# The last 64 gate rows and the last 64 up rows of an FFN share one chunk of TensorE's columns

## What is computed

```
DIM = 256;  HID = 704;  ZERO_POINT = 128.0
def _qlinear(x, wq, scale):
    W = (wq.astype(jnp.float32) - ZERO_POINT) * scale[:, None]
    return jnp.einsum('bsd,hd->bsh', x, W)
gate = jax.nn.silu(_qlinear(x, wq_gate, s_gate))
up = _qlinear(x, wq_up, s_up)
return _qlinear(gate * up, wq_down, s_down)
...
x = _layernorm(x + _L0_ffn_ref(x, ...), axis=-1)
```

## Time and profile before

| | us |
|---|---|
| three runs | 2053.20, 2056.19, 2057.21 |
| median of the runs | 2056.19 |
| the profiled execution: span from first to last instruction | 2053.5 |
| TensorE busy in it | 1911.6 (93% of the span) |
| VectorE busy | 1560.7 (76%) |
| ScalarE busy | 1052.1 (51%) |

### The profile page before, as it was taken

One profiled execution on the slowest core, in us unless ns is written; L12 is line 12 of the kernel. 1 busy time (PEld: TensorE's weight loads), 2 busy tenths in 40 slices (PEclk: granted clock), 3 DMA queues, 4 the chain that ended last, 5 costly groups with the idle time before them and its releaser, 6 DMA issues. The chain is left out here.

```text
span 2053.5 us, 36820 instructions
## 1 busy us (share of the span) xinstructions
PE 1911.6 (93%) x12560; PEld 1717.0 (84%) x12560; DVE 1560.7 (76%) x4280; ACT 1052.1 (51%) x2677; POOL 839.0 (41%) x865
## 2 busy tenths in 40 slices
PE   7999999999999969999799999999999999977981
PEld 6888888888888858888689999999999999977981
DVE  7978778777787755565478888888888888865656
ACT  5434333333433333322377666666666666634753
POOL 1222323233232310000144466666666666744776
PEclk9999999999999989999799999999999999998995
DMA  3200000010000222743000010000000000126867
GB/s 123 83 1 32 21 11 32 1 32 1 32 21 1 75 77 92 256 143 124 19 12 17 19 41 24 20 20 19 19 18 19 18 18 13 38 71 168 197 136 250
DMA packets 101928, 118.81 MB, mean 58 GB/s; under 512 B 12552, under 2 KB 93644, under 8 KB 101105
## 3 DMA queue, kind: packets, MB, share of 16 engines
q1 hardware_dynamic: 89024, 108.35, 16.3%
q0 software_dynamic: 12288, 8.11, 2.6%
q10 hardware_dynamic: 432, 0.02, 0.0%
HBM read 75.43 MB, written 57.10 MB: 65 GB/s over the span
## 5 line engine op out<-in xcount | busy, mean ns | idle before, releaser
L237 POOL TENSOR_TENSOR rwkv_gate<-rwkv_key,rwkv_gate 128x512 f32<-128x512 f32 x128 | 203.6, 1591 | 525.7 <-DVE rwkv_key L442 525.7
L1419 POOL TENSOR_TENSOR kept_raw<-kept_raw,mla_row_inv 128x512 f32<-128x512 f32 x192 | 199.2, 1037 | 302.1 <-DVE mla_row_inv L1771 300.7
L310 ACT ACTIVATE rwkv_gate<-rwkv_r 128x512 f32<-128x512 f32 x128 | 76.7, 599 | 400.7 <-DVE rwkv_o_low L363 398.0
L1576 ACT ACTIVATE kept_raw<-kept_raw,mla_least 128x256 f32<-128x256 f32 (+1 forms) x512 | 227.8, 446 | 90.8 <-DVE mla_least L1755 89.8
L1755 DVE CUSTOM_DVE_ANT_0 kept_raw<-mla_score,kept_mask 128x256 f32<-128x256 f32 (+1 forms) x512 | 156.8, 352 | 80.0 <-PE mla_score L2130 79.5
L427 DVE TENSOR_TENSOR rwkv_kv<-rwkv_v,rwkv_key 128x512 f32<-128x512 f32 x128 | 88.0, 687 | 125.8 <-PE rwkv_v L475 123.6
L434 DVE TENSOR_TENSOR_SCAN rwkv_state<-rwkv_decay_w,rwkv_kv 128x256 f32<-128x256 f32 x256 | 166.0, 691 | 4.1
L2130 PE MATMUL mla_score<-mla_k_high,mla_q_high 128*128 128x256 f32 (+1 forms) x512 | 155.3, 303 | 0.0
L492 PE MATMUL rwkv_out<-rwkv_w_high,rwkv_o_high 128*128 128x256 f32 x512 | 143.3, 280 | 5.8 <-DVE rwkv_o_low L363 5.8
L492 PE MATMUL rwkv_out<-rwkv_w_high,rwkv_o_low 128*128 128x256 f32 x512 | 144.6, 282 | 0.0
L492 PE MATMUL rwkv_out<-rwkv_w_low,rwkv_o_high 128*128 128x256 f32 x512 | 143.5, 280 | 0.0
(11 more groups left out here) (403 smaller groups left out, 6417.4 us busy)
## 6 DMA issues: line engine op xcount, KB each, us to landing
kept_raw<-in_experts SPq DMA_DIRECT2D x27, 384.0 KB
kept_raw<-in_rkvo SPq DMA_DIRECT2D x16, 512.0 KB
moe_y_in<-sums SPq DMA_DIRECT2D x32, 256.0 KB, 4.6
sums<-ffn_empty SPq DMA_DIRECT2D x12, 512.0 KB
slots<-ffn_empty SPq DMA_DIRECT2D x16, 361.2 KB
moe_e_rows<-slots SPq DMA_DIRECT2D x32, 180.6 KB
kept_x_in<-x SPq DMA_DIRECT2D x18, 256.0 KB, 2.7
mla_x_res<-x SPq DMA_DIRECT2D x17, 256.0 KB
```

The costliest lines, as they stand in the source:

```text
L237: nc.gpsimd.tensor_tensor(gate[:, c % 2, :], key[:, c % 2, :], gate[:, c % 2, :], ALU.mult).then_inc(gated_done, 1)
L1419: nc.gpsimd.tensor_tensor(unit, unit, row_inv[:, v % PR, 0:len(heads)].rearrange("p (h a) -> p h a", a=1) .to_broadcast([P, len(heads), ke ...
L1576: last = nc.scalar.activation(probs[:, v % PR, i * keys:(i + 1) * keys], masked[:, v % 2, i * keys:(i + 1) * keys], ACT.Exp, bias=least[:, ...
```

## The change

The gate weights' sixth chunk is filled: its first 64 columns are the last 64 gate rows as before, its other 64 columns are the last 64 up rows. One projection of 6 matmuls then gives both, gate rows in lanes 0 to 63 and up rows in lanes 64 to 127 of one bank, and the up projection of j = 5 is gone. For this chunk ScalarE reads lanes 0 to 63 and writes its gate into lanes 64 to 127; `hidden` and `h_high` are made in lanes 64 to 127, and VectorE writes the low part of hidden not into `h_low` but into lanes 0 to 63 of `h_high`. The down weights of this chunk are loaded twice, into both halves of the lanes; the low weights' first half is zero. So one matmul with the high weights gives high by high plus low by high, one with the low weights gives high by low: 2 matmuls per token tile in place of 3. TensorE gets one new wait: at j = 1 the gate projection also waits for the `hidden` of chunk 5, which now reads the gate bank. Three memsets go and one comes, and the splitting of the up weights and of the down weights is done in two pieces each.

The diff, without the declaration and the waits of the removed semaphore `padded` and without the count that SyncE waits for at the end of the phase before:

```diff
@@ -211,7 +211,9 @@
                 sp.wait_ge(w_low_done, CH)
                 sp.dma_start(code_down[:, 0:HC - 1, :], wq_down[0:(HC - 1) * P, :].rearrange("(c p) d -> p c d", p=P))\
                     .then_inc(next_in, 16)
-                sp.dma_start(code_down[0:HTAIL, HC - 1, :], wq_down[(HC - 1) * P:HID, :]).then_inc(next_in, 16)
+                for half in range(2):
+                    sp.dma_start(code_down[half * HTAIL:(half + 1) * HTAIL, HC - 1, :], wq_down[(HC - 1) * P:HID, :])\
+                        .then_inc(next_in, 16)
                 sp.wait_ge(m_high_done, 3 * NB)
                 sp.wait_ge(m_low_done, 3 * NB)
                 for i in range(2):
...
@@ -604,6 +605,14 @@
         mult_high = s.sem("mult_high")
         mult_low = s.sem("mult_low")
 
+        def gate_lanes(j):
+
+            return slice(0, P) if j < HC - 1 else slice(0, HTAIL)
+
+        def hidden_lanes(j):
+
+            return slice(0, P) if j < HC - 1 else slice(HTAIL, P)
+
         def products(g):
             return hid_ps[g % 2][0], hid_ps[g % 2][1]
 
...
@@ -684,17 +693,20 @@
         def _(act):
             def w_high(part):
                 act.wait_ge(centred_done, part + 1)
-                if part < 2 * KD:
-                    i, k = part // KD, part % KD
-                    out, src = w_part[0][:, i, k, 0:HID], centred[:, i, k, :]
+                if part < KD:
+                    last = nc.scalar.activation(w_part[0][:, 0, part, 0:HID], centred[:, 0, part, :], ACT.Copy)
+                elif part < 2 * KD:
+                    k = part - KD
+                    nc.scalar.activation(w_part[0][:, 1, k, 0:HID - HTAIL], centred[:, 1, k, 0:HID - HTAIL], ACT.Copy)
+                    last = nc.scalar.activation(w_part[0][:, 0, k, HID:HPAD], centred[:, 1, k, HID - HTAIL:], ACT.Copy)
                 else:
-                    out, src = wd_part[0][:, :, :], centred_down[:, :, :]
-                nc.scalar.activation(out, src, ACT.Copy).then_inc(w_high_done, 1)
+                    last = nc.scalar.activation(wd_part[0][:, :, :], centred_down[:, :, :], ACT.Copy)
+                last.then_inc(w_high_done, 1)
 
             def xt_high(blk, par):
                 act.wait_ge(transposed, blk + 1)
                 if not (isinstance(blk, int) and blk < 2):
-                    act.wait_ge(up_ready, HC * (blk - 1))
+                    act.wait_ge(gate_ready, HC * (blk - 1))
                 for k in range(KD):
                     nc.scalar.activation(xt_part[0][:, par, k, :], xt_ps[k][:, :], ACT.Copy)\
                         .then_inc(xt_high_done, 1)
...
@@ -702,7 +714,8 @@
             def h_high(n, j):
                 act.wait_ge(hidden_done, n + 1)
                 wait_reuse(act, step_out_done, n, 2)
-                nc.scalar.activation(h_part[0][:, j % 2, :], hidden[:, j % 2, :], ACT.Copy)\
+                lanes = hidden_lanes(n % HC)
+                nc.scalar.activation(h_part[0][lanes, j % 2, :], hidden[lanes, j % 2, :], ACT.Copy)\
                     .then_inc(h_high_done, 1)
 
             w_high(0)
...
@@ -737,8 +750,9 @@
                         attention_high()
                     act.wait_ge(gate_ready, n + 1)
                     wait_reuse(act, hidden_done, n, 2)
-                    nc.scalar.activation(gate[:, j % 2, :], hid_ps[j % 2][0][:, :], ACT.Silu,
-                                         scale=scale_hid[:, 0, j:j + 1]).then_inc(gate_done, 1)
+                    rows_of = gate_lanes(j)
+                    nc.scalar.activation(gate[hidden_lanes(j), j % 2, :], hid_ps[j % 2][0][rows_of, :], ACT.Silu,
+                                         scale=scale_hid[rows_of, 0, j:j + 1]).then_inc(gate_done, 1)
                     if j == 4 and not last:
                         xt_high(blk + 1, 1 - par)
                     if not (first and j == 0):
...
@@ -769,9 +782,10 @@
 
             def h_low(n, j):
                 dve.wait_ge(h_high_done, n + 1)
-                nc.vector.tensor_tensor(h_part[1][:, j % 2, :], hidden[:, j % 2, :],
-                                        h_part[0][:, j % 2, :].bitcast(F32), ALU.subtract)\
-                    .then_inc(h_low_done, 1)
+                lanes = hidden_lanes(n % HC)
+                out = h_part[1][:, j % 2, :] if n % HC < HC - 1 else h_part[0][0:HTAIL, j % 2, :]
+                nc.vector.tensor_tensor(out, hidden[lanes, j % 2, :], h_part[0][lanes, j % 2, :].bitcast(F32),
+                                        ALU.subtract).then_inc(h_low_done, 1)
 
             def layer_norm(blk):
 
...
@@ -809,13 +823,18 @@
 
             def w_low(part):
                 dve.wait_ge(w_high_done, part + 1)
-                if part < 2 * KD:
-                    i, k = part // KD, part % KD
-                    out, src, high = (w_part[1][:, i, k, 0:HID], centred[:, i, k, :],
-                                      w_part[0][:, i, k, 0:HID])
+                if part < KD:
+                    pieces = [(w_part, (slice(None), 0, part, slice(0, HID)), centred[:, 0, part, :])]
+                elif part < 2 * KD:
+                    k = part - KD
+                    pieces = [(w_part, (slice(None), 1, k, slice(0, HID - HTAIL)), centred[:, 1, k, 0:HID - HTAIL]),
+                              (w_part, (slice(None), 0, k, slice(HID, HPAD)), centred[:, 1, k, HID - HTAIL:])]
                 else:
-                    out, src, high = wd_part[1][:, :, :], centred_down[:, :, :], wd_part[0][:, :, :]
-                nc.vector.tensor_tensor(out, src, high.bitcast(F32), ALU.subtract).then_inc(w_low_done, 1)
+                    full, tail = (slice(None), slice(0, HC - 1)), (slice(HTAIL, P), HC - 1)
+                    pieces = [(wd_part, full, centred_down[full]), (wd_part, tail, centred_down[tail])]
+                for of, at, src in pieces:
+                    last = nc.vector.tensor_tensor(of[1][at], src, of[0][at].bitcast(F32), ALU.subtract)
+                last.then_inc(w_low_done, 1)
 
             centre(0)
             centre(1)
...
@@ -826,9 +845,7 @@
             centre(3)
             w_low(2)
             w_low(3)
-            nc.vector.memset(code_down[HTAIL:P, HC - 1, :], int(ZERO_POINT)).then_inc(padded, 1)
-            for i in range(2):
-                nc.vector.memset(w_part[i][:, :, :, HID:HPAD].bitcast(F32), 0.0).then_inc(padded, 1)
+            nc.vector.memset(wd_part[1][0:HTAIL, HC - 1, :].bitcast(F32), 0.0)
             centre(4)
             w_low(4)
             dve.wait_ge(consts_in, 16 * 3)
...
@@ -864,12 +881,14 @@
                     if blk == PREP + 1 and j == 4:
                         attention_low()
 
-                    dve.wait_ge(up_ready, n + 1)
+                    if j < HC - 1:
+                        dve.wait_ge(up_ready, (HC - 1) * blk + j + 1)
                     dve.wait_ge(gate_done, n + 1)
                     wait_reuse(dve, h_low_done, n, 2)
-                    nc.vector.scalar_tensor_tensor(hidden[:, j % 2, :], hid_ps[j % 2][1][:, :],
-                                                   scale_hid[:, 1, j:j + 1], gate[:, j % 2, :],
-                                                   ALU.mult, ALU.mult).then_inc(hidden_done, 1)
+                    lanes = hidden_lanes(j)
+                    up = hid_ps[j % 2][1 if j < HC - 1 else 0]
+                    nc.vector.scalar_tensor_tensor(hidden[lanes, j % 2, :], up[lanes, :], scale_hid[lanes, 1, j:j + 1],
+                                                   gate[lanes, j % 2, :], ALU.mult, ALU.mult).then_inc(hidden_done, 1)
                     if j == 4 and not last:
                         xt_low(blk + 1, 1 - par)
                     if not (first and j == 0):
...
@@ -907,12 +926,14 @@
                     pe.wait_ge(xt_high_done, KD * (blk + 1))
                     pe.wait_ge(xt_low_done, KD * (blk + 1))
                 for i, (ready, read) in enumerate(((gate_ready, gate_done), (up_ready, hidden_done))):
-                    if first and j == 0:
-                        pe.wait_ge(w_high_done, KD * (i + 1))
-                        pe.wait_ge(w_low_done, KD * (i + 1))
-                    if first and j == HC - 1:
-                        pe.wait_ge(padded, 3)
+                    if first and (j == 0 or (j == HC - 1 and i == 0)):
+                        pe.wait_ge(w_high_done, KD * (i + 1 if j == 0 else 2))
+                        pe.wait_ge(w_low_done, KD * (i + 1 if j == 0 else 2))
+                    if j == HC - 1 and i == 1:
+                        break
                     wait_reuse(pe, read, n, 2)
+                    if j == 1 and i == 0 and not first:
+                        pe.wait_ge(hidden_done, n - 1)
                     for q, (wp, xp) in enumerate(PARTS):
                         for k in range(KD):
                             last = nc.tensor.matmul(hid_ps[j % 2][i][:, :],
...
@@ -932,14 +953,15 @@
                         pe.wait_ge(w_low_done, 2 * KD + 1)
                 elif j == 0:
```

(8 more changed lines are left out.)

4 lines of the change are left out of this document (1 added, 3 removed).

## The result

The changed kernel takes 2044.37 us (median of 4 runs, 2040.85 to 2047.52), the kernel before, on the same chip, 2054.69 (4 runs): a ratio of 0.995, with a 95% interval of 0.9938 to 0.9961, so 8 to 13 us less. The forecast was 2048.6 us within 2043.5 to 2053; the sign and the range held, and the gain was about 2.7 us more than the 7.6 forecast; the other 1.5 us of the distance to 2048.6 is the kernel before, whose median over four runs lies that much under the one over three. The profiled execution took 2044.34 us, with a span of 2042.0 (before: 2053.5).

The account below looks back on a forecast made before the run. TensorE was taken to set the FFN's pace; 8.1 + 0 + 1.07 + 1.0 = 10.2 us gained, less 2.6 for the clock, gave 7.6 us: 2056.2 - 7.6 = 2048.6 us, range 2043.5 to 2053.

Parts of the forecast that it names:

- What is removed: Chunk 5 of each block: six up and four down matmuls fewer, 1.83 us per block, 14.6 us gross.
- The wait at step_out(3): Blocks 0 to 6: TensorE waits there for h_low(3), losing 0.21 us and leaving 1.62 of 1.83 in ordinary blocks.
- The 0.15 until a result reaches TensorE: From the end of h_low to the matmul using it, read at block 7's end and applied to step_out(3): 0.15 us.
- The start of block 0: Splitting weights in two pieces ahead of gate(0): taken as 0, between 0.6 us gained and 0.4 lost.
- The saving of block 3 meets a transfer: Block 3's 1.62 us only lengthen block 4's wait for rows, 1.33 to 2.95 us; worth 0.
- Block 4: TensorE waits 0.76 us for h_low(3), made late behind the attention weights' split; 1.07 us left of 1.83.
- The clock: Block 4's 2.95 us idle drops the clock for 6.8 us: 3.4 lost, less 0.76 no longer waited, 2.6 us.
- rival B: The clock holds through block 4's wait: 10.2 us gained, 2046.0 us; chance 24%.
- Block 7: FFN's end: gate matmuls' end to step_out(4) takes 2.52 us, 0.82 of 1.83 lost, 1.0 us left.
- The new wait at j = 1: TensorE waiting for hidden(5) costs nothing: done at about 856.7, asked for at 860.6, 3.9 us of cover.
- Rival E: Cross-lane writes or reading `h_high` written by two engines far dearer; at 7.5 us, 0.5 lost per block, 2060; chance 4%.
- Rival C: Phases behind the FFN eat most of the gain: 0.8 to 4.2 us gained, around 2053.5; chance 15%.

Follow-up runs that it names:

- e5: Changed kernel with both engines making the parts of hidden(3) ahead of those of the next block's x at j = 4: 2044.62 us, 0.9951 to before.
- e6_filler: Changed kernel with 13 matmuls that nothing reads in the wait for block 4's rows: 2043.14 us, 0.9947 to before.
- e8_before_more_dma: Kernel before with only the change's second load of 64 down rows added, in the phase ahead: 2052.89 us, 0.9999 to before.
- e3_spread: Changed kernel with the four attention head loads spread over blocks 3 to 6, one each: 2038.20 us, 0.9926 to before.
- after_again: The changed kernel run once more, unedited: 2044.81 us, 0.9961 to before.
- e1_three_down: Changed kernel with chunk 5's down product again three matmuls per token tile, on lanes 64 to 127: 2050.05 us, 0.9979 to before.
- e9: Changed kernel with chunk 5's high-by-low product added twice, three matmuls of 128 lanes per token tile: 2048.67 us, one run, time not used.

## Why the prediction was right, step by step

| part of the FFN | forecast us | measured us |
|---|---|---|
| start to the residual load of block 1 | -1.62 | -1.19 |
| blocks 1 and 2 | -3.24 | -3.24 |
| blocks 3 and 4 with the clock | +1.5 | +0.98 |
| blocks 5 and 6 | -3.24 | -3.20 |
| block 7 to the next phase | -1.0 | -1.40 |
| sum | -7.6 | -8.05 |

**What is removed: right.** 1.83 us a block; e5 shows it bare (25.69 - 23.86).

**The wait at step_out(3): right, 0.21 us,** shown by the timeline of block 5 and by e5. In some blocks up to 0.16 us more goes with it (24.21 in e6_filler), which the forecast did not have. "The 0.15 until a result reaches TensorE", read at the end of block 7, held elsewhere too.

**The start of block 0, costed at nothing: three things in one.** The first row of the table is 0.43 us short. Most of it isn't TensorE's time. Timelines of before, then of the changed kernel, where the residual load of block 2 is issued:

```profile
817.36 0.28 PE L938 MATMUL ffn_out<-ffn_wd_high,ffn_h_high 128*128 128x256 f32 x1
817.39 0.36 SPq L642 DMA_DIRECT2D ffn_x_res<-x  x1
```

```profile
815.04 0.28 PE L960 MATMUL ffn_out<-ffn_wd_high,ffn_h_high 128*128 128x256 f32 x1
815.39 0.36 SPq L651 DMA_DIRECT2D ffn_x_res<-x  x1
```

The load now comes 0.36 us behind the first matmul of step_out(0) instead of 0.03, in nearly every block. So 0.33 of the 0.43 is the measuring mark, which has moved against TensorE; the last row of the table has it back. To that matmul the start is 1.52 us shorter, 0.10 less than forecast. One part of that is seen: the up projection waits 0.36 us for the last `w_low` (758.84, above), which is made in two pieces now, in all nine profiles with the change (0.13 in the three without). But the clock counts for more. At the start of the FFN it is still at the lower level, and when it rises differs between executions. Windows over the first 12 us of the stage, in before, e8_before_more_dma, the changed kernel and e3_spread (seventh number the granted clock):

```profile
750.36:762.36 12.00, 9.43 (x32) 6.89 (x32) 9.37 (x15) 6.79 (x9) 0.06 (x1) 0.67 0.59 189
750.72:762.72 12.00, 9.43 (x29) 7.12 (x30) 9.37 (x15) 6.79 (x9) 0.06 (x1) 0.59 0.80 183
751.19:763.19 12.00, 9.19 (x28) 6.92 (x29) 9.49 (x16) 7.52 (x12) 0.06 (x1) 0.58 0.78 192
750.60:762.60 12.00, 9.19 (x32) 6.87 (x32) 9.49 (x16) 7.51 (x11) 0.07 (x1) 0.66 0.83 193
```

0.67 is 8 us at the lower level, 0.58 is 10. In the kernel before this makes no difference: 41.35 us to the residual load of block 1 with either, since the wait of 0.64 us for the gate is there with the early rise and gone with the late one. In the changed kernel it makes 0.5: 39.60 in e3_spread with the early rise, 40.16, 40.16 and 40.09 in the changed kernel, after_again and e6_filler with the late one. So with an early rise the start gained 2.0 us to that matmul, 0.4 more than forecast, and with a late one 1.5. Which execution gets which is not the change's doing as far as these profiles tell: both kernels show both.

**The saving of block 3 meets a transfer: the mechanism right, the size not.** e3_spread takes the transfers away, and block 3's share comes back (24.10 us). The wait grew by 2.59 us, not 1.62. Of the 0.97 us more, 0.33 is that the residual load of block 3, which begins the stretch, comes later against TensorE (see block 0); TensorE's own work in it was 0.14 longer than forecast, which takes some of that back; and 0.78 is that the stretch from this load to the transposes wasn't 32.7 us but 33.45 (839.46 to 872.91). In the nine profiles with the loads in one piece it lay between 32.5 and 34.1: 32.67 and 32.54 in the two with the old chunk 5, 33.36 to 34.06 in the seven with the new one (33.51 when the changed kernel was run again). "It runs at the pace of the transfers" is thus true, but I had taken this pace for a constant. Why it is 0.7 to 1.4 us longer with the change stays open. In the changed kernel the residual load of block 4 is issued right behind the rows (864.72), before it came 4.4 us behind them, so the two small loads may share what the heads leave; no run separates this, and in e8, where it came 2.8 us behind them, the stretch was 32.54.

**Block 4: hidden.** The 0.76 us for h_low(3) don't appear where TensorE runs at the lower clock, as the text took into account; e6_filler shows them with the clock up, at 0.61.

**The clock: the step that was mis-sized.** It did fall (rival B is out), but for 3.5 us and not 6.8, in both profiles of the changed kernel. I chose the middle of three sizes seen in other phases, for no better reason. That the sum came within half a microsecond is in part luck: the clock cost 1.7 us less than forecast (0.9 for 2.6), and the longer wait took about 1.0 more (2.59 for 1.62). It was 3.5 us in the five profiles with waits of 2.6 to 4.0 us, 6.7 after 4.5, none after 1.2 and 1.3. In this kernel it was worth less still, since half of it was hidden: 0.9 us of FFN by e6.

**Block 7: right.** 2.54 us against 2.52. The 0.4 by which the last row differs lies ahead of it: from the last residual load to step_out(3) it was 12.37 us before (947.61 to 959.98) and 10.68 after (941.79 to 952.47), 1.69 less where the up matmuls make 1.37. The other 0.32 is the residual load's new place, 0.33 us later against TensorE (above), and gives back what the first row lost.

**The new wait at j = 1, costed at nothing: right.** TensorE never waits at j = 1: in block 5 the silu of chunk 5 starts at 905.29, 0.07 behind step_out(3), and hidden(5) is done 1.5 us later, long before TensorE asks. Rival E has no row.

**Beyond the FFN.** The FFN gives 8.05 us, and the timed difference was 10.3 in one comparison and 8.7 in the other. Rival C, a gain eaten later, did not come. What went the other way is not traced to its cause: e8 rules out the added load, and the last stage, which gave 3.9 of the 11.5 us between the first two spans, is shorter in all nine profiles with the change than in the three without (see e8), with nothing that connects them. So of the 2.7 us beyond the forecast 0.45 is the FFN's, and the other 2.3 stay open: spread of the later phases, or an effect of the change on them that the forecast did not have. In the second comparison (8.7 us, with 8.0 in the FFN) what lies outside the FFN is 0.7 us.

## What to carry to other kernels

- A matmul taken out is worth its distance between starts, and this adds up exactly (1.83 us a block here) where TensorE paces; add up the places where a transfer paces apart from these, since there the gain turns into a wait, and the wait can cost clock besides. Spreading the loads that stand ahead of a small one in the queue was worth 5.5 us of FFN after the change and 1.8 before it, so such a repair should be tried again after each speed-up.
- Half-full chunks are worth merging: two halves in one projection (1.16 us a block here), and the low part of a split number in the free lanes, so that one pass of the contraction adds two products (0.46).
- A distance between two marks is only as good as the marks. A load that moved by 0.33 us against TensorE looked like a loss at one end of the FFN and like a gain at the other; measure from the engine that sets the pace.
- A stretch at the pace of transfers is not a constant: take it from several executions, or give it a microsecond of range.

## What the runs showed of the hardware

- Going from weights of 128 rows to weights of 64 and back costs 0.4 us (0.20 going and 0.20 coming back in the rows of e1_three_down, and 0.30 to 0.44 between the distances of e1 and e9), while within a row of either kind the distance of matmuls of 256 columns is the same 0.115 to 0.117 us. On the way there the weight load wasn't issued ahead of the matmul.
- Matmuls that nothing reads, put into a wait of 3.9 us, kept the clock at 1.00 with 1.2 us of idle time left (e6_filler), for 0.9 us of gain.
- ScalarE writes to lanes 64 to 127 what it reads in lanes 0 to 63 at no extra time (0.69 us for 512 columns, 0.69 in place), and so does VectorE from lanes 64 to 127 to lanes 0 to 63 (0.69 us, 0.68 in place).
- A clock that rose 2 us later at the start of the FFN cost nothing in the kernel before, where TensorE then had no wait of 0.64 us for ScalarE, and 0.5 us in the changed one (41.35 and 41.35 us before, 39.60 and 40.16 after).
